# Layer 3's 4-bit feed-forward: two batches rounded together, with GpSimd taking the differences

## The reference

```
def fake_quant_nvfp4(x, global_scale):
    xb = x.reshape(sh[:-1] + (sh[-1] // BLOCK, BLOCK))
    amax = jnp.max(jnp.abs(xb), axis=-1, keepdims=True)
    sc = jnp.clip(amax / FP4_MAX * global_scale, 0.0, FP8_MAX)
    sc8 = sc.astype(jnp.float8_e4m3fn).astype(jnp.float32)
    dq = sc8 / global_scale
    safe_dq = jnp.where(dq == 0.0, 1.0, dq)
    a = jnp.clip(jnp.abs(xb) / safe_dq, 0.0, FP4_MAX)
    q = jnp.sign(xb) * _FP4_VALS[jnp.digitize(a, _FP4_MIDS)]
    return (q * dq).reshape(sh)
...
gate_out = nvfp4_linear(x, gate_w, s_in[0])
up_out = nvfp4_linear(x, up_w, s_in[0])
hidden = jax.nn.silu(gate_out) * up_out
return nvfp4_linear(hidden, down_w, s_in_down[0])
```

## Time and profile before

| What | us |
|---|---|
| Median of 3 runs (2362.84 to 2365.53) | 2364.27 |
| The profiled execution's own time | 2364.53 |
| Its span, first to last instruction | 2363.2 |
| First gated product to the last difference in the last stage | 89.75 |
| From there to the end of the span | 11.40 |

### The profile page before, as it was taken

How to read it: one execution, slowest core, us unless ns; L and a number is a source line. 1 busy time by engine, 2 the same in 40 slices (tenths; PEclk the granted TensorE clock), 3 DMA queues, 4 the chain that set the end, 5 groups by cost and what they waited for, 6 DMA issues and landing times.

```text
span 2363.2 us, 57229 instructions
## 1 busy us (share of the span) xinstructions
PE 2043.6 (86%) x22720; PEld 1483.5 (63%) x22720; DVE 1354.9 (57%) x3605; ACT 883.8 (37%) x3421; POOL 500.9 (21%) x1131
## 2 busy tenths in 40 slices
PE   7999999998987799897976887999999998789843
PEld 3788888786656566465865654666554544556522
DVE  5666666674335688544644633787263210678797
ACT  2344444443236466211333532666210111246511
POOL 3344444221001100101324511332000000411111
PEclk9655555799989899799997998999999999789966
DMA  3000000104000000300011000000030000000000
GB/s 133 3 5 5 5 4 5 75 2 175 3 1 2 14 12 5 134 1 23 1 48 81 2 1 7 11 8 5 1 148 0 1 0 1 1 14 15 2 0 16
DMA packets 7752, 57.20 MB, mean 24 GB/s; under 512 B 760, under 2 KB 5216, under 8 KB 5728
## 3 DMA queue, kind: packets, MB, share of 16 engines
q1 hardware_dynamic: 7488, 53.54, 5.9%
HBM read 52.62 MB, written 0.92 MB: 23 GB/s over the span
## 4 chain that ended last, share of the span: by engine, by line
PE 66%; DVE 14%; issue 9%; ACT 6%; POOL 4%; DMA 1%; DVEq 0%; POOLq 0%; ACTq 0%; SPq 0%
PE banks L259 42%; PE banks L264 8%; PE banks L1323 6%; PE banks L908 3%; ACT memory L956 2%; DVE memory L1421 2%; PE banks L934 2%; ACT memory L1352 1%; PE banks L1474 1%; ACT memory L1359 1%; DVE memory L1218 1%; DVE memory L795 1%; DVE memory L1427 1%; DVE memory L1430 1%; DVE memory L1439 1%
## 5 line engine op out<-in xcount | busy, mean ns | idle before, releaser
L259 PE MATMUL banks<-memory 128*112 128x256 f32 (+7 forms) x4192 | 1134.2, 427 | 70.7 <-ACT memory L3444 8.0
L259 PEld LDWEIGHTS banks<-memory 128*128 128x128 f32 (+3 forms) x4192 | 708.2, 196 | 401.5 <-issue 258.9
L264 PE MATMUL banks<-memory 112*125 112x112 f32 (+3 forms) x2000 | 305.9, 286 | 123.7 <-DVE memory L795 66.7
L264 PEld LDWEIGHTS banks<-memory 112*125 112x125 f32 (+3 forms) x2000 | 238.6, 172 | 240.3 <-issue 142.9
L1323 PE MATMUL banks<-memory 128*128 128x8 bf16 (+2 forms) x10752 | 325.9, 175 | 25.6 <-DVE memory L1439 5.8
L1323 PEld LDWEIGHTS banks<-memory 128*128 128x128 bf16 x10752 | 304.2, 104 | 48.0 <-DVE memory L1439 45.9
L956 ACT ACTIVATE memory<-banks,memory 112x375 f32<-112x375 f32 x384 | 215.4, 579 | 19.5 <-DVE memory L994 19.1
L994 DVE TENSOR_REDUCE memory<-banks 112x2 f32<-112x750 f32 x192 | 171.0, 933 | 37.0 <-PE banks L908 36.8
L811 POOL TENSOR_TENSOR memory<-memory 112x1 f32<-112x1 f32 x72 | 39.6, 550 | 416.1 <-DVE memory L790 414.6
L1002 DVE COPY memory<-banks 125x448 f32<-125x448 f32 x192 | 116.8, 619 | 11.3 <-PE banks L264 6.9
L1421 DVE TENSOR_REDUCE memory<-banks 128x48 f32<-128x192 f32 x448 | 109.4, 286 | 5.5 <-PE banks L1323 5.5
(11 more groups left out here) (233 smaller groups left out, 2403.8 us busy)
## 6 DMA issues: line engine op xcount, KB each, us to landing
memory<-in_l2x SPq DMA_DIRECT2D x1, 7680.0 KB, 21.5
memory<-in_l2f SPq DMA_DIRECT2D x1, 7168.0 KB, 19.8
memory<-in_l1f SPq DMA_DIRECT2D x1, 4617.0 KB, 14.1
memory<-in_ctxT SPq DMA_DIRECT2D x24, 187.5 KB
memory<-in_l0a SPq DMA_DIRECT2D x1, 4224.0 KB, 16.5
memory<-in_l2f SPq DMA_DIRECT2D x1, 4096.0 KB, 12.8
memory<-in_l3f SPq DMA_DIRECT2D x1, 3073.0 KB, 22.5
memory<-in_l2a SPq DMA_DIRECT2D x1, 3072.0 KB, 18.4
```

The costliest lines, as they stand in the source:

```text
L259: ins = self.nc.tensor.matmul(out, weights[i], acts[i], start=i == 0, stop=i == n - 1)
L264: return self.nc.tensor.transpose(out, in_, self.ident[0:n, 0:n])
```

## The change

`order()` becomes a list over four pairs of batches. VectorE now does for each pair p of batches 2p and 2p + 1:

- "hid": the gated product of one batch, and behind it at once that batch's block maxima (`dve_hidden`).
- "scale": the nine scale operations once for both, 128 wide, and the multiplication by the inverse scales, 2048 wide. From the second pair on it waits for an older unit (`quant_ready(2 * i)`).
- "range": the three range operations, 2048 wide.
- "round": two additions, 1024 wide each, which signal `sums_ready`.

The gated product (with maxima) of batch 2p + 2 stands between "scale" and "range" of pair p, that of batch 2p + 3 between "range" and "round". The two sums of the pair before follow "round". GpSimd does the difference of each unit from unit 1 to unit 8 (L3455 of the new file), waits for it with `gstep`, and does the product as before. Unit 0's difference stays on VectorE. The last unit's difference and product (batch 7) are both VectorE's, and TensorE waits for it on the new semaphore `last_ready`. y, t, scales, the hidden rows and hT are there twice, and units use banks 4 and 5 in turn. TensorE turns batches 2p - 2 and 2p - 1 beside pair p: one before and one after the projection of batch 2p + 3. The last two batches are turned behind all else. The second row unit is turned only behind the first four batches' projections.

```diff
     def order(self):
...
-        for b in range(B):
-            yield "four", b + 2
-            if b + 1 < B:
-                yield "gate", b + 1
-            if b:
-                yield "sum", b - 1
+        yield "hid", 0
+        yield "gate", 1
+        yield "hid", 1
+        for p in range(HALF):
+            last = p == HALF - 1
+            yield "scale", p
+            if not last:
+                yield "gate", 2 * p + 2
+                yield "hid", 2 * p + 2
+            if p:
+                yield "turn", 2 * p
+            if not last:
+                yield "gate", 2 * p + 3
+            yield "turn", 2 * p + 1
+            yield "range", p
+            if not last:
+                yield "hid", 2 * p + 3
+            yield "round", p
+            if p:
+                yield "sum", 2 * p - 2
+                yield "sum", 2 * p - 1
+        for b in (B - 2, B - 1):
             yield "turn", b + 2
-        yield "sum", B - 1
+        for b in (B - 2, B - 1):
+            yield "sum", b
...
+    def dve_hidden(self, b):
+        k, s, V = self.k, self.s, self.nc.vector
+        hid = self.half(self.hids, b + 2)
+        V.wait_ge(*s.silu_ready(b + 1))
+        V.scalar_tensor_tensor(
+            out=hid.rearrange("p (h n) -> p h n", h=2), in0=k.banks[0:S, 2:4, :], scalar=self.inv[0:S, 1:2],
+            in1=self.sg.rearrange("p (h n) -> p h n", h=2), op0=ALU.mult, op1=ALU.mult).then_inc(*s.hid_ready.up())
+        V.wait_ge(*s.hid_ready(b + 1))
+        four_bit_tops(k, hid, self.scales(b + 2)[:, 0])
+
+    def dve_round(self, n, whole):
+
+        k, s, V = self.k, self.s, self.nc.vector
+        y, t = self.half(self.y, n), self.half(self.t, n)
+        V.wait_ge(*s.vstep.now())
+        if not whole:
+            V.tensor_tensor(y, y, t, ALU.add).then_inc(*s.sums_ready.up())
+            return
+        V.tensor_tensor(y, y, t, ALU.add).then_inc(*s.vstep.up())
+        V.wait_ge(*s.vstep.now())
+        V.tensor_tensor(y, y, t, ALU.subtract).then_inc(*s.sums_ready.up())
+        if n == self.LAST:
+            V.wait_ge(*s.sums_ready(n + 1))
+            V.wait_ge(*s.tp16_full(n - 1))
+            four_bit_values(V, self.values[n % 2], y, self.scales(n)[:, 1]).then_inc(*s.last_ready.up())
+
     def pool(self):
...
+        for n in range(self.LAST):
+            y = self.half(self.y, n)
+            G.wait_ge(*s.sums_ready(n + 1))
+            if n:
+                G.tensor_tensor(y, y, self.half(self.t, n), ALU.subtract).then_inc(*s.gstep.up())
+                G.wait_ge(*s.gstep.now())
+            if n >= 2:
+                G.wait_ge(*s.tp16_full(n - 1))
+            four_bit_values(G, self.values[n % 2], y, self.scales(n)[:, 1]).then_inc(*s.quant_ready.up())
...
     def pe_turn(self, n, read):
         k, s, PE = self.k, self.s, self.nc.tensor
-        PE.wait_ge(*s.quant_ready(n + 1))
-        k.fill(bank, read)
+        PE.wait_ge(*(s.last_ready(1) if n == self.LAST else s.quant_ready(n + 1)))
+        k.fill(4 + n % 2, read)
```

More of the change, by code:

```diff
@@ L147, in __init__ @@
         self.sums_ready = new("sums_ready")
+        self.last_ready = new("last_ready")
         self.xl_ready = new("xl_ready")
@@ L3308, in __init__ @@
         self.ident16 = take(P, dt=BF16)
-        self.y, self.t = [take(HID, parts=S) for _ in range(2)], take(HID, parts=S)
-        self.sc = [take(3, HID // 16, parts=S) for _ in range(2)]
+        two = lambda *dims, dt=F32: [take(*dims, dt=dt, parts=S) for _ in range(2)]
+        self.hids, self.y, self.t = two(2 * HID), two(2 * HID), two(2 * HID)
+        self.sc = two(3, 2 * HID // 16)
         self.xT = four_bit_rows(k)
-        self.values = [take(HID, dt=BF16, parts=S) for _ in range(2)]
@@ L3313, in __init__ @@
-        self.sg, self.hids = take(HID, parts=S), take(2, HID, parts=S)
-        self.hT = take(8, S, dt=BF16)
+        self.values = two(HID, dt=BF16)
+        self.sg = take(HID, parts=S)
+        self.hT = [take(8, S, dt=BF16) for _ in range(2)]
     def order(self):
         yield "norm", B - 1
-        yield "four", 0
-        yield "four", 1
+        yield "rows", 0
+        yield "rows", 1
         yield "turn", 0
         yield "gate", 0
-        yield "turn", 1
-        for b in range(B):
-            yield "four", b + 2
-            if b + 1 < B:
-                yield "gate", b + 1
-            if b:
-                yield "sum", b - 1
-            yield "turn", b + 2
@@ L3354, in dve @@
                 norm_row_stats(k, i, st, s.stat_ready)
-            elif step == "gate":
-                V.wait_ge(*s.silu_ready(i + 1))
-                V.scalar_tensor_tensor(
-                    out=self.hids[:, i % 2, :].rearrange("p (h n) -> p h n", h=2), in0=k.banks[0:S, 2:4, :],
-                    scalar=self.inv[0:S, 1:2], in1=self.sg.rearrange("p (h n) -> p h n", h=2), op0=ALU.mult,
-                    op1=ALU.mult).then_inc(*s.hid_ready.up())
-            elif step == "four":
-                kind, b = self.UNITS[i]
-                if kind == "hidden":
-                    V.wait_ge(*s.hid_ready(b + 1))
-                elif b:
-                    V.wait_ge(*s.xn_ready(1))
-                if i >= 2:
-                    V.wait_ge(*s.quant_ready(i - 1))
-                src, gs = self.rows_of(i)
-                four_bit_scales(k, src, gs, self.sc[i % 2])
-                four_bit_sums(k, src, self.y[i % 2], self.t, self.sc[i % 2])
-                V.wait_ge(*s.vstep.now())
-                V.tensor_tensor(self.y[i % 2], self.y[i % 2], self.t, ALU.subtract).then_inc(*s.sums_ready.up())
+            elif step == "rows":
+                if i:
+                    V.wait_ge(*s.xn_ready(1))
+                src = k.row_norms[:, i * HALF:(i + 1) * HALF, :].rearrange("p b d -> p (b d)")
+                y, t = self.half(self.y, i), self.half(self.t, i)
+                four_bit_scales(k, src, w["s_in"][0:S, 0:1], self.scales(i))
+                four_bit_scaled(k, src, y, self.scales(i))
+                four_bit_range(k, y, t)
+                self.dve_round(i, i == 0)
+            elif step == "hid":
+                self.dve_hidden(i)
+            elif step == "scale":
+                sc = self.sc[i % 2]
+                if i:
+                    V.wait_ge(*s.quant_ready(2 * i))
+                four_bit_steps(k, w["s_in"][0:S, 1:2], sc)
+                four_bit_scaled(k, self.hids[i % 2], self.y[i % 2], sc)
+            elif step == "range":
+                four_bit_range(k, self.y[i % 2], self.t[i % 2])
+            elif step == "round":
+                self.dve_round(2 * i + 2, False)
+                self.dve_round(2 * i + 3, 2 * i + 3 == self.LAST)
             elif step == "sum":
```

67 lines of the change are left out of this document (34 added, 33 removed).

## The result

| What | before | after |
|---|---|---|
| Median, us (lowest to highest; 4 runs each) | 2364.90 (2362.84 to 2366.11) | 2378.78 (2376.85 to 2380.41) |
| Profiled execution's own time, us | 2364.53 | 2380.41 |
| Its span, us | 2363.2 | 2379.1 |
| First instruction of the last stage (a cast by VectorE) | 2240.92 | 2248.07 |
| From there to the end of the last sum | 117.35 | 126.10 |

The ratio is 1.0057, with an interval of 1.0041 to 1.0073: slower, by 13.9 us between the medians. The forecast was 2372.4, and the time lies 0.8 us above the top of the range. The table splits the 15.9 us between the spans of the two profiled executions in three: 7.15 in code ahead of the stage, which the change doesn't touch; 8.75 in the stage, forecast at 8.1; nothing behind it.

The account below looks back on a forecast made before the run. VectorE was taken to bound the last stage (busy 85.55 of 89.75 us). Each pair saves 5.0 us but stalls 6.4; with idle time at start and end, 8.1 us longer: 2372.4 us, range 2365.5 to 2378.

Parts of the forecast that it names:

- Passes: Last stage, between first additions of successive pairs: 23.9, 23.9 and 19.0 us, where two batches took 22.54.
- GpSimd's difference: Last stage, 1024 f32 values in place on GpSimd: taken as 2.19 us, from a line between two traced sizes.
- Small operations held by GpSimd: VectorE's scale operations in each pass: four get in between GpSimd's operations, at about 2 us each.
- End, last pair's first addition to last sum: End of the last stage: additions, differences, product, transposes, copies and projections take 14.4 us.
- The mechanism: Last stage: VectorE's two-input or number operations and GpSimd's alternate in asking order, stalling VectorE 6.4 us for each pair.
- no lock: Rival for the last stage: GpSimd holds nothing up, passes are 17.5, 17.5 and 12.7 us, total 2351.6; chance 0.10.
- VectorE keeps its turn: Rival: GpSimd enters only beside reciprocal, products and maxima; stall about 2.4 us a pass, total 2360.4 to 2364; chance 0.09.
- slower still: Rival: GpSimd's difference takes 2.6 us and gated products come tenths late; total 2376 to 2378; chance 0.05.
- the upper bound that I had named: In the forecast's own range, GpSimd's difference at 2.35 us instead of 2.19, which adds 1.1 us.
- the forecast's 6.21: Start of the last stage: 6.21 us from first to second gated product, VectorE idle for 3.6 of them.
- the line that gave 2.19: Estimate of GpSimd's 1024-value difference, on the line between 4080 ns for 2048 values and 1134 ns for 448.

Follow-up runs that it names:

- e8: The changed kernel as it is, measured a third time: 2373.64 us against 2363.80 for the kernel before, ratio 1.0035.
- e4: The changed kernel with all differences on VectorE, GpSimd only multiplying: ratio 1.0021 to the kernel before, stage 121.51 us.
- e3: The changed kernel with the next pair's second gated product and maxima moved behind the two additions: ratio 1.0007 to the kernel before, stage 119.95 us.
- e6: The changed kernel with GpSimd's eight differences left out, so its output is wrong: ratio 0.9981 to the kernel before, stage 111.16 us.
- e7: New version of the changed kernel: single batches at both ends, three pairs between, differences on VectorE, product and sums behind them: 2356.88 us against 2364.98 before.
- e2: The changed kernel as it is, measured again: 2376.37 us, ratio 1.0037 to the kernel before, stage 126.15 us.
- e5: The kernel before with only the differences of batches 0 to 6 given to GpSimd: 2364.36 us against 2364.98, stage 119.35 us.

## Why the prediction was right, and where it failed

| Step | Forecast | Measured |
|---|---|---|
| First gated product, after the start of the stage | 1.14 earlier | 19.94 against 21.13: 1.19 earlier |
| From it to the second gated product | 6.21, VectorE idle for 3.6 | 5.84, idle for 3.31 (e8: 6.24, idle for 3.71) |
| From it to the end of pair 0's first addition | 24.26 | 23.99 |
| Passes | 23.9, 23.9, 19.0 | 24.24, 24.24, 19.33 |
| GpSimd's difference; the first of a pair, which waits | 2.19; 3.1 | 2.35; 3.27 |
| Small operations held by GpSimd | four a pass, about 2 each | 1.59, 2 x 2.13, 1.97 |
| End, last pair's first addition to last sum | 14.4 | 14.35 |
| Stage | +8.1 | +8.75 (9.35 in e8) |

**The mechanism was right**: VectorE's two-input and number operations and GpSimd's exclude each other and alternate. The excess over the free lengths (0.29, 0.49 for two, 0.23, as e4 and after itself show them) is 1.30 + 3.78 + 1.74 = 6.8 us a pass, forecast at 6.4. The rule that I took from the Trainium skill, "SBUF — State Buffer", section "Who interferes with whom", is borne out by after, e3, e4, e6 and e7. The rivals are out: "no lock" wanted passes of 17.5 and small operations at their usual length; "VectorE keeps its turn" allowed 2.4 us of stall, where 6.8 are measured; "slower still" wanted a difference of 2.4 or more and gated products that come too late, where the difference is just below and no gated product after the second waits. That its 2376 to 2378 us came nearest to the first measurement is luck.

**The mis-sized term** is GpSimd's difference: 2.35, the upper bound that I had named, not 2.19. It stands twice in each of three passes and once at the end, 0.16 x 7 = 1.1 us. The shorter idle time at the start gives 0.4 back, and that is luck with the clock: in e8, with the clock at 0.50 as in before, the forecast's 6.21 is met (6.24) and the stage costs 9.35. The Trainium skill's 4497 ns for 2048 values ("GPSIMD Engine Reference", section 3.1) had led to 2.25 because I halved it; put on the line that gave 2.19, it gives an estimate of 2.34. The measurement decides: 2.35.

**The step that failed** is the one from the stage to the whole time. "I read the busy time of the last stage first, because the change touches nothing else"; the stage's 8.1 us were then added to the median of three runs of before (2362.84 to 2365.53) as if the rest took a fixed time; and "A measurement of this kernel can tell about 0.2% (4.7 us) from no change." That the change touches nothing else is true. But untouched code isn't code of fixed time. Over the ten profiles the same work ahead of the stage ended between 2237.1 and 2248.1, and 30 runs of before lie between 2360.85 and 2373.40. The range had a term for every uncertain price in the stage and none for this. In the profiled execution of the first measurement that term was 7.15 us, against the stage's 8.75.

What the first measurement's 13.9 us hold beside the stage is less sure. The repeats give 8.8 us (5.4 to 12.3; e2) and 8.3 us (5.4 to 11.1; e8), near the stage's own 8.75 to 9.35, and in the table of experiments the stage predicts the ratio to 1.7 us for all kernels but this first one, where some 5 us are left over. Its interval (9.7 to 17.3 us) still overlaps those of the repeats. But its four runs of after, 2376.85 to 2380.41, lie high together: of the 18 later runs of the same kernel 15 are below 2376.85 and none is above 2378.73. One of the four was profiled and had its 7.15 us ahead of the stage; of the other three nothing is known. Both repeats, with medians of 2376.37 and 2373.64, lie within the forecast's range.

I can't say why the low stretch falls on different work: the rows show that it does, and in the first profile of after, in e2 and in e6 the stage came 5 to 7 us later than in before's, while e8, the same kernel as e2, had none of it. What sets its moment was not tried, and the cause stays open.

One assumption was never put to an experiment, that the reciprocal goes beside GpSimd. The trace of before has a place that bears it out (timelines of GpSimd and VectorE):

```profile
989.97 1.13 POOL L2894 TENSOR_TENSOR memory<-memory 128x448 f32<-128x448 f32 x1 [1.68 <-ACT memory L2885]
...
990.34 0.20 DVE L2749 RECIPROCAL memory<-memory 112x8 f32<-112x8 f32 x1
990.57 0.61 DVE L2731 TENSOR_TENSOR memory<-memory 112x64 f32<-112x64 f32 x1
```

GpSimd works until 991.10. The reciprocal lies wholly beside it at its usual 0.20 us, and the operation on two memory tiles behind it is held until 991.18. That is the small form; the wide one (0.95 us) lies beside no GpSimd operation in any pass.

## What to carry to other kernels

Before an elementwise operation goes to GpSimd, look at what VectorE does in that time: what GpSimd takes has to lie beside VectorE work that GpSimd doesn't hold up. Lay the product from PSUM, the maxima and the sums behind the hand-over, and the small chained operations elsewhere (e3 and e7 against after); and look who waits for the result, since GpSimd is also the slower of the two (e5). In no run here did handing over the differences pay against before: the stage was longer by 2.0 us (e5), 2.6 (e3) and 8.75 (after). A chain of tiny VectorE operations is a bad neighbour, since each of them can be held for a full GpSimd operation. Where a change moves a stage by 0.3%, read its cost from the stage's own length in the profile, and give the rest of the program a term in the range, sized from many runs.

## What the runs showed of the hardware

- The two engines alternate one for one: an operation of GpSimd that waits goes ahead of VectorE's next, and the other way round. The 128-wide operations that are held take 1.15 to 2.15 us in the rows above, where 0.23 to 0.29 is their length, and the wait counts as busy time on both engines.
- A waiting operation needs less once it is let in: GpSimd's difference that was asked for 1.06 us early took 3.27, that is 2.21 from the release, against 2.34 to 2.35 alone. That its start-up lay in the wait is my reading of it.
- Free beside GpSimd, at full length: a product that reads PSUM and one tile (1.28), the maxima (1.21 to 1.22), the sums (0.87 for two) and a reciprocal of 112x8 (0.20).
- On GpSimd an in-place difference of 112x1024 f32 values takes 2.35 us, and the product with a broadcast scale into bf16 1.93, so the difference, with two full f32 inputs and an f32 output, is the slower. Which of these makes it so was not tried.
- The granted TensorE clock falls to 0.50, over whole windows of 6 and of 8 us in the rows above, at different moments in executions of the same code. Where such a stretch lay 8 us later, what follows came 3.9 us later. The 30 runs of before lie 12.5 us apart; whether all of that is the clock wasn't traced.
